# Expert layers: slots filled by rows gathered from a token table, in place of rows scattered to their slots

## What is computed

```python
x = hidden_states.reshape(-1, H)                  # 1024 x 256
logits = x @ w_gate                               # 8 experts
logits = SOFTCAP * jnp.tanh(logits / SOFTCAP)
probs = jax.nn.softmax(logits, axis=-1)
_, idx = jax.lax.top_k(probs, TOPK)               # the best 2 of 8
mask = jax.nn.one_hot(idx, E, dtype=probs.dtype).sum(-2)
weights = probs * mask
for e in range(E):
    h = jax.nn.silu(x @ w1[e]) * (x @ w3[e])      # 256 -> 512
    out = out + h @ w2[e] * weights[:, e:e + 1]   # 512 -> 256
```

## Time and profile before

| What | Value |
|---|---|
| Time, median of 3 runs | 2636.81 us (2633.54 to 2636.89) |
| Profiled execution, own time | 2635.1 us |
| Its span, first to last instruction | 2633.0 us |
| Mean granted clock of TensorE | 0.857 of full |
| First expert layer | about 62 to 257 us of the span |
| Second expert layer | about 359 to 554 us |
| TensorE busy in one expert layer | 146.3 us of 195 |
| Last slot index known to first tile transposed | 24.6 us, in either layer |

### The profile page before, as it was taken

How to read it: one execution, slowest core, us unless ns; L and a number is a source line. 1 busy time by engine, 2 the same in 40 slices (tenths; PEclk the granted TensorE clock), 3 DMA queues, 4 the chain that set the end, 5 groups by cost and what they waited for, 6 DMA issues and landing times. The chain is left out here.

```text
span 2633.0 us, 45240 instructions
## 1 busy us (share of the span) xinstructions
PE 2078.7 (79%) x16876; PEld 1605.9 (61%) x16888; DVE 1525.1 (58%) x3266; ACT 1180.3 (45%) x2905; POOL 1044.7 (40%) x965
## 2 busy tenths in 40 slices
PE   8497438978887995967798577976789676779798
PEld 5365225646565874756587466865668665546686
DVE  2222642236675335787876876868778678357432
ACT  3211421126364333853566545655556555236433
POOL 0222012220002542586535864368623767100254
PEclk9698768989998997967799588996789777989799
DMA  8422013210003303321322213222122221120430
GB/s 288 132 24 48 9 39 71 25 44 2 23 2 97 142 0 70 106 73 33 113 80 78 69 50 100 89 63 81 57 89 81 67 69 65 37 55 2 126 113 16
DMA packets 138317, 179.47 MB, mean 68 GB/s; under 512 B 62048, under 2 KB 114544, under 8 KB 132992
## 3 DMA queue, kind: packets, MB, share of 16 engines
q1 hardware_dynamic: 129952, 166.46, 20.4%
q0 software_dynamic: 8160, 10.26, 2.5%
HBM read 154.52 MB, written 22.17 MB: 67 GB/s over the span
## 5 line engine op out<-in xcount | busy, mean ns | idle before, releaser
L2695 DVE SCALAR_TENSOR_TENSOR XT<-M_delta,CW_delta,XT 128x256 f32<-128x256 f32 x576 | 249.0, 495 | 67.7 <-ACT M_delta L2475 39.7
L2146 PE MATMUL PS<-XP_delta,X 128*128 128x268 f32 (+1 forms) x1024 | 247.2, 395 | 19.8 <-DMA X<-in_L_attn_b_heads 15.6
L2146 PEld LDWEIGHTS PS<-XP_delta,X 128*128 128x128 f32 x1024 | 196.0, 193 | 71.8 <-DMA X<-in_L_attn_b_heads 19.8
L1541 PE MATMUL PS<-XP_rffn,UW_rffn 128*128 128x512 f32 x816 | 195.3, 396 | 4.6 <-POOL UW_rffn L1495 4.6
L1541 PEld LDWEIGHTS PS<-XP_rffn,UW_rffn 128*128 128x128 f32 x816 | 156.4, 192 | 38.4 <-issue 5.4
L1273 ACT ACTIVATE PR_attn<-PS,NM_attn 128x256 f32<-128x256 f32 (+1 forms) x384 | 130.8, 448 | 103.5 <-DVE NM_attn L1343 103.5
L1495 POOL TENSOR_TENSOR UW_rffn<-W_rffn,UW_rffn 128x512 fp32r<-128x512 f32 x34 | 43.7, 1286 | 301.5 <-ACT UW_rffn L1602 301.5
L561 POOL DMA_INDIRECT sums<-XS_moe,token_moe x46 | 71.7, 1559 | 221.4 <-ACT XS_moe L661 207.0
L2613 ACT ACTIVATE S_delta<-S_delta,AO_delta 128x128 f32<-128x128 f32 x512 | 159.5, 393 | 0.0
L1663 DVE TENSOR_TENSOR SU_rffn<-PS,CB_rffn 128x512 f32<-128x512 f32 x68 | 47.0, 691 | 179.4 <-PE PS L1541 157.0
L2177 PE MATMUL PS<-KQ_delta,TR_delta 128*128 128x64 f32 x1024 | 133.8, 275 | 9.6 <-ACT TR_delta L2540 8.4
(11 more groups left out here) (459 smaller groups left out, 5259.5 us busy)
## 6 DMA issues: line engine op xcount, KB each, us to landing
M_delta<-gram_delta SPq DMA_DIRECT2D x32, 1280.0 KB, 6.0
X<-in_L_attn_b_heads SPq DMA_DIRECT2D x64, 512.0 KB, 3.5
EW<-in_L_ffn_w SPq DMA_DIRECT2D x24, 512.0 KB, 10.0
CB_rffn<-routes_rffn SPq DMA_DIRECT2D x20, 512.0 KB, 21.9
XN<-in_L_attn_b_outs SPq DMA_DIRECT2D x16, 512.0 KB, 3.7
F_delta<-in_L_attn_b_outs SPq DMA_DIRECT2D x4, 2048.0 KB, 9.5
W_rffn<-in_L_ffn_tiles SPq DMA_DIRECT2D x4, 1536.0 KB, 11.5
slots<-pad SPq DMA_DIRECT2D x2, 2967.0 KB, 14.1
```

Of the source, the lines that this page charges most:

```text
L1541: last = nc.tensor.matmul(PS[:, 4 + 2 * n + q, :], UW[qw][:, r, (q * KD + k) * P:(q * KD + k + 1) * P], XP[qx][:, k, n * NB:(n + 1) * NB], ...
L2146: last = nc.tensor.matmul(PS[:, 1 + i, 0:B * (WIN - halo)], WH[:, r, i, k, :], XP[:, k, :, n * BT + halo:n * BT + WIN], start=(k == 0), st ...
L2695: nc.vector.scalar_tensor_tensor(TMP[:, r, i], RAW[:, r, i, :, tau:tau + BT], CW[:, i, h, tau:tau + 1], TMP[:, r, i], ALU.mult, ALU.add).t ...
```

## The change

`setup`, `load_experts` and `moe` change; a class `Routing` takes over the bookkeeping. `slots` is gone. XN itself is written to a tensor `rows` in HBM (1024 rows and 128 padding rows of zeros), and each tile is gathered from there by an indirect DMA that reads 128 rows by their number. For that the kernel needs a table: for each of the 128 places (lanes) in each of the 23 tiles, which token is there, and its weight. It is made as a matrix product: `spread` holds, for each of 16 columns of pairs, a 128 x 128 one-hot of the lane, `entry` a row of 23 + 23 values that are zero except at the pair's tile (row number and weight), and 16 products `spread[:, j]` x `entry[:, j]` add up the table in PSUM.

```diff
@@ load_experts
-        self.fill_slots(sp)
-        sp.dma_start(self.sums[N:N + P], self.pad[:, 0:D]).then_inc(self.zeroed, 16)
+        sp.dma_start(self.rows[N:N + P], self.pad[:]).then_inc(self.zeroed, 16)
+        sp.dma_start(self.sums[N:N + P], self.pad[:]).then_inc(self.zeroed, 16)
@@ class Routing (new): TensorE
+    def table(self, pe, spread):
+        w = (1 + self.weighted) * self.TILES
+        pe.wait_ge(self.entry_d, 1)
+        for j in range(2 * NT):
+            pe.wait_ge(self.spread_d, j // NT + 1)
+            last = nc.tensor.matmul(PS[:, 6, P:P + w], spread[:, j], self.entry[:, j].rearrange("p x t -> p (x t)"),
+                                    start=j == 0, stop=j == 2 * NT - 1)
+        last.then_inc(self.table_mm, 1)
+    def experts(self, pe):
+        pe.wait_ge(self.owner_d, 1)
+        return [pe.value_load(self.owner[0:1, t:t + 1], min_val=0, max_val=E - 1) for t in range(self.TILES)]
@@ class Routing: VectorE, behind `where` in place()
+        c.then(nc.vector.tensor_tensor(self.at_least, by_slot(self.where).broadcast_to([P, 2 * NT, t + 1]),
+                                       self.tile_at[:].unsqueeze(1).broadcast_to([P, 2 * NT, t + 1]), ALU.is_ge))
+        c.then(nc.vector.tensor_reduce(self.tiles_up[:], self.at_least, AX.X, ALU.add))
+        c.then(nc.vector.scalar_tensor_tensor(self.lo[:], self.tiles_up[:], -float(P), self.where[:], ALU.mult, ALU.add))
+    def spread(self, dve, spread, half):
+        nc.vector.tensor_tensor(spread[:, h], self.lane[:].unsqueeze(1).broadcast_to([P, NT, P]),
+                                self.lo[:, h].unsqueeze(2).broadcast_to([P, NT, P]), ALU.is_equal).then_inc(self.spread_d, 1)
+    def entries(self, dve, c):
+        nc.vector.scalar_tensor_tensor(self.value[:]..., ALU.mult, ALU.add)
+        c.then(nc.vector.tensor_tensor(self.in_tile, self.at_least[:, :, 0:t], self.at_least[:, :, 1:t + 1], ALU.subtract))
+        last = nc.vector.tensor_tensor(self.entry[:, :, 0], self.in_tile, over(self.value[:]), ALU.mult)
+        if self.weighted:
+            last = nc.vector.tensor_tensor(self.entry[:, :, 1], self.in_tile, ..., ALU.mult)
+        last.then_inc(self.entry_d, 1)
+    def tokens(self, dve, c):
+        dve.wait_ge(self.table_mm, 1)
+        if self.weighted:
+            nc.vector.tensor_copy(self.share[:], PS[:, 6, P + t:P + 2 * t])
+        c.then(nc.vector.tensor_tensor(self.token_f[:], PS[:, 6, P:P + t], self.own[:].broadcast_to([P, t]), ALU.add))
+        nc.vector.tensor_copy(self.token[:], self.token_f[:]).then_inc(self.token_d, 1)
@@ moe, SyncE
+            norm.rows_ready(sp)
+            sp.dma_start(rows, XN[:]).then_inc(rows_out, 16)
             sp.wait_ge(g_in, 16)
-            sp.wait_ge(placed, 32 * NT * (layer_no + 1))
-            for i in range(len(GROUPS) - 1):
-                at = slice(GROUPS[i], GROUPS[i + 1])
-                sp.dma_start(XS[:, at], slots[:, at]).then_inc(x_in[i], 16)
-            if layer_no == 0:
-                core.fill_slots(sp)
@@ moe, GpSimd
-            for i in range(NT):
-                for r in range(2):
-                    nc.gpsimd.indirect_dma_start(
-                        core.slots[:], bass.IndirectOffsetOnAxis(ap=slot[:, r, i:i + 1], axis=0),
-                        XW[:, r, i], None).then_inc(placed, 16)
+            def gather(t):
+                nc.gpsimd.indirect_dma_start(XS[:, t], None, core.rows[:],
+                                             bass.IndirectOffsetOnAxis(ap=token[:, t:t + 1], axis=0)).then_inc(x_in[t], 16)
+            pool.wait_ge(rows_out, 16)
+            pool.wait_ge(routing.token_d, 1)
+            for t in range(AHEAD):                      # AHEAD = 6
+                gather(t)
             for t in range(TILES):
                 pool.wait_ge(y_ev, t + 1)
                 if t or layer_no:
                     pool.wait_ge(added, 16 * (TILES * layer_no + t))
                 nc.gpsimd.indirect_dma_start(core.sums[:], ...token[:, t:t + 1]..., XS[:, t], None, compute_op=ALU.add)
+                if t + AHEAD < TILES:
+                    gather(t + AHEAD)
@@ moe, TensorE
+            routing.ranks(pe)
+            e = routing.experts(pe)
+            routing.table(pe, spread)
@@ moe, ScalarE
             norm.scalar(act)
-            norm.rows_ready(act)
-            nc.scalar.copy(XW[:, 0, :, 0:D], XN[:])
-            nc.scalar.copy(XW[:, 1, :, 0:D], XN[:]).then_inc(rows_d, 1)
+            act.wait_ge(routing.token_d, 1)             # behind exp, ahead of the loop
@@ moe, VectorE
+            routing.choose(dve, c, prob)
+            routing.place(dve, c)
+            routing.spread(dve, spread, 0)
+            routing.entries(dve, c)
+            routing.spread(dve, spread, 1)
+            routing.owners(dve, c)
+            routing.tokens(dve, c)
```

More of the change, by code:

```diff
@@ L472, in moe @@
     prob = s.sb("prob", [P, NT, E])
[L473 to L499 removed]
+    mx = s.sb("mx", [P, NT])
+    XS = s.sb("XS", [P, TILES, D])
+    spread = s.sb("spread", [P, 2 * NT, P])
     XK = s.sb("XK", [P, 3, KD, P])
@@ L676, in _ @@
             c = Chain(dve, chain_v)
-            for e in range(E):
-                nc.vector.memset(rank[:, e:e + 1], float(E - e))
-                last = nc.vector.memset(edges[:, e:e + 1], float(P * e))
-            for t in range(TILES):
-                last = nc.vector.memset(tile_at[:, t:t + 1], float(P * t))
-            c.then(last)
+            routing.tables(dve, c)
             dve.wait_ge(tanh_d, 1)
@@ L694, in _ @@
-            c.then(nc.vector.tensor_reduce(weight[:], chosen[:], AX.X, ALU.add))
-            nc.vector.tensor_copy(XW[:, :, :, D + 1], weight[:])
-            for r in range(2):
-                last = nc.vector.tensor_copy(XW[:, r, :, D], core.row_id[:, 0:NT])
-            last.then_inc(rows_d, 1)
-            dve.wait_ge(sum_mm, 1)
-            dve.wait_ge(consts, 2)
-            c.then(nc.vector.tensor_reduce(count[:], PS[:, 6, 0:NT * E].rearrange("p (i e) -> p e i", e=E), AX.X, ALU.add))
-            c.then(nc.vector.tensor_tensor(over[:], count[:].unsqueeze(2).broadcast_to([P, E, E]),
-                                           edges[:].unsqueeze(1).broadcast_to([P, E, E]), ALU.is_gt))
@@ L711, in _ @@
-            c.then(nc.vector.tensor_tensor(chosen[:], oh[:], place[:].unsqueeze(1).broadcast_to([P, 2, NT, E]), ALU.mult))
-            c.then(nc.vector.tensor_reduce(where[:], chosen[:], AX.X, ALU.add))
-            nc.vector.tensor_copy(slot[:], where[:]).then_inc(slot_d, 1)
-            c.then(nc.vector.tensor_tensor(past[:], tile_at[:].unsqueeze(2).broadcast_to([P, TILES, E - 1]),
-                                           base[:, 1:E].unsqueeze(1).broadcast_to([P, TILES, E - 1]), ALU.is_ge))
```

241 lines of the change are left out of this document (144 added, 97 removed).

## The result

| | Before | After |
|---|---|---|
| Time, median of 8 runs each | 2635.93 us (2632.6 to 2641.01) | 2643.39 us (2638.73 to 2649.43) |
| Span of the profiled execution | 2633.0 us | 2645.2 us |
| First / second expert layer, first load of one stage to first load of the next | 195.63 / 196.08 us | 202.56 / 202.69 us |
| End of `where` to first transpose, layer 1 | 24.6 us | 33.1 us |

The change made the kernel slower: after over before is 1.0039, 95% interval 1.0027 to 1.005, some 10 us (7 to 13); the two medians of the table are 7.5 us apart. 2651 was forecast, with 2641 to 2660 as the range. The two layers together are 13.5 us longer in the profiled executions (14.8 forecast); the rest of the program differs by 1.3 us the other way.

A forecast was written before the change was run, and what follows sets the result against it. The prediction took TensorE's products to bound the loop, and the wait for the first tile's transpose to decide the change. Terms sum to +7.4 us a layer, +14.8 for two, on 2635.1: 2649.9, taken as 2651 us, range 2641 to 2660.

The forecast's parts named there:

- Ahead of `where`: Before `where`, ScalarE's two copies into XW and the copies of weight and row number go: -0.8 us a layer.
- VectorE to `owner`: Behind `where`, VectorE's new operations, with `owner` last of all, add 6.1 us a layer.
- Register loads: On TensorE's queue between ranks and table, 23 loads lose their cover and add their full 15.2 us a layer.
- Table: On TensorE, 16 fp32 products, two instructions each, at half clock: +7.3 us a layer, bounds 4.2 to 8.4.
- Tokens: Behind the table, three small VectorE operations, chained once: +0.5 us a layer.
- First gather: From GpSimd's start, through the first indirect DMA, to the first transpose: +3.5 us a layer, bounds 2.6 to 4.9.
- Removed: Behind `where`, the scatters, their landing and the load back go: -24.6 us a layer.
- Second gather: Follows the first by 1.26 to 1.5 us, where the second tile came 1.24 later: +0.2 us a layer.
- rival D: Register loads run beside products and don't hold up the table, so the kernel isn't slower: 2627 us; chance 4%.
- B: The table's products bring TensorE's clock up before the loop, saving 3.5 to 4 us a layer: 2643 us; chance 14%.
- C: GpSimd's queue becomes the loop's bound as adds wait for gathers: some 2682 us, mild form 2655 to 2662; 12% for both.
- Signs forecast for the trace: Table starts when register loads end, takes 7.3 us at 0.50; first gather 0.8 us later; tiles stay 5.6 us apart.

The follow-up runs named there:

- table first with one load: Changed kernel with the table's products ahead of the register loads and one load instruction for all 23 registers; 2607.0 us, 0.9913 of before.
- loads spread: Changed kernel with tiles' experts computed right behind `where`, six register loads ahead of the table, seven behind, ten in the loop; 2612.0 us, 0.9926 of before.
- `owner` early: Changed kernel with VectorE computing the tiles' experts right behind `where`, so register loads can start earlier; 2632.5 us, 1.0004 of before.
- uncovered loads: Kernel before with one more wait: its 23 register loads also wait for the first group of XS; 2664.9 us, 1.0124 of before.
- paced gathers: Changed kernel with all 23 gathers ahead of the adds, each from the seventh waiting until the previous landed; 2671.9 us, 1.0143 of before.

## Why the prediction was right

*The path.* The prediction held that the layer's length hangs on when the first tile can be transposed. In all kernels whose loop is undisturbed the layer moves with that moment: 16.8 us sooner gives 16.8 us less (table first with one load, against after), 16.3 gives 16.7 (loads spread). (The moment is counted from `where`; a slower router, see the last section, comes on top.)

*Term by term*, layer 1, forecast and then what the rows of after show:

| Step | Forecast | Measured | From |
|---|---|---|---|
| Ahead of `where` | -0.8 | -0.6 | `where` ends 19.45 us after the stage's start (63.31), before 20.01 (62.02); the router took 4.46 us, before 4.22 |
| VectorE to `owner` | 6.1 | 6.2 | 82.76 to 89.0 |
| Register loads | 15.2 | 15.2 | 89.0 to 104.18 |
| Table | 7.3 | 7.0 | 7.03, at 0.50 |
| Tokens | 0.5 | 0.5 | 111.21 to 111.73 |
| First gather | 3.5 | 4.1 | 111.73 to 115.85 |
| Removed | -24.6 | -24.6 | |
| First tile | +7.2 | +7.9 | 52.54 us after the stage's start, before 44.61 |
| Second gather | +0.2 | 0.0 | second tile 1.27 us behind the first, before 1.27 |
| The layer | +7.4 | +6.9 | 202.56 - 195.63 |

The step on which the sign rests, register loads that lose their cover, is shown from three sides: they stand in the open in after, they make the kernel before slower by 1.2% when they are uncovered there, and the changed kernel is faster than before as soon as they are shortened, spread or put behind the table.

*The terms that were mis-sized.* The first gather: GpSimd starts 0.93 us after `token` has ended, where I took 0.3 from waits for a short VectorE operation; from its start to the transpose it took 3.19, as composed. Against that stands something the sum had at nothing: the half clock at the loop's start lasts 5.3 us behind the first transpose, before 6.7, which gives 0.7 us of TensorE time back. That isn't the table's doing: in `owner` early, whose two layers have the same code, it lasts 4.6 and 6.8 us. So this part of the agreement is luck. These two leave +7.2, and 6.9 was measured; the last 0.3 us weren't traced.

*Whole program.* Two layers give +13.5. The stage ahead of the first layer is 1.3 us longer in the profiled execution of after and a later feed-forward stage 4.4 us shorter. The 1.3 us are 16 transposes near the start that took 3.67 us in after, as long as the same ones at 0.50, and before 2.31; the profile has the granted clock at 1.00 there in both, so what made them longer stays open. Of the change the stage has only `load_experts`, without its filling of `slots`. The feed-forward stage holds nothing of it. The other stages make up 1.8 more, and the spans differ by 12.2. Over all runs it is 10.3 us (7.1 to 13.2), below my 14.8 by more than the layers of the profiled execution explain. Where the rest lies can't be read: only one execution of each kernel is traced, and that of after took 2647.0 us, 3.6 above its median. Two small slips are in the total: 2649.9 and 1.7 make 2651.6, and rival D's 2627 leaves the 1.7 out.

*Rivals.* B fell: the clock is 0.50 from the table to the first tiles in after, and with the table issued twice as well. C fell in the loop: a gather adds 0.1 us to an add's cycle. Another form of it, all 23 gathers in a row, does cost 17 us a layer, by a mechanism I hadn't named and no run shows. D, loads that run beside products, was false for this order but not in its mechanism: the loads do run beside products, those ahead of them on the queue. I had argued "one queue, in order" as if an instruction's end, not its issue, let the next one go; for the order that was forecast both read alike, for the reversed order it was wrong by 5 us (22.6 in place of 27.5).

*Signs forecast for the trace.* L540 begins when the register loads end (104.18 after 104.1), takes 7.0 at 0.50, the loop begins at 0.50, adds don't wait for DMA in it but for the last of each layer: all as written. The tiles are 5.8 apart in the middle of the loop and 5.6 at its end; I had read the 5.6 off the last adds of before, whose middle has 5.8 as well.

## What to carry to other kernels

When a change removes a long wait, list what else stood under it: here 15 us of register loads cost nothing beneath the scatters and became the largest term on the path. Put queue work such as register loads behind products that are already issued, never ahead of ones that others wait for; one swapped line turned this change from 0.4% slower to 0.3% faster, and with one load instruction for all registers to 0.9% faster. A row of indirect DMAs that is long and unbroken should be looked at in the trace, even where each of them is early.

## What the runs showed of the hardware that was not expected

- Register loads run beside products ahead of them on TensorE's queue: the first load starts at 89.0 while the table's products end at 93.0.
- A load of 23 registers takes 2.1 to 2.3 us as one instruction. Each register's operation and assertion takes about 0.29 us more, 6.6 us in all.
- The granted clock stayed 0.50 through 13.86 us of unbroken products of 46 columns, and fell from 1.00 within such products when wide ones (512 columns) had raised it.
- Single register loads took 0.30 us beside direct loads of some 350 GB/s, and up to 0.92 us right after the filling of `slots` had been started.
- ScalarE and VectorE stood still for 14 to 17 us beside 23 unbroken gathers, and not beside 17, though the stall begins when no more than 15 have been issued. Beside 12, VectorE stood still for 1.5 us in one layer and up to 2.7 in the other.
- The router's 32 instructions, which took 4.22 us before, took 6.96 to 6.97 in five layers of kernels that don't change them: the first layer with the uncovered loads and with the table issued twice, the second of `owner` early, and both with the paced gathers. One of them:

```profile
73.08 6.97 PE L700 MATMUL PS<-WG_moe,XT 128*128 128x8 f32 x32 [0.72 <-DVE XT L245]
```

  In `owner` early the clock was 0.50 through all of its second layer's router products, and in its first layer (4.07 us) it fell only near their end. So the clock moves a layer's length by close to 3 us with no change in the work; differences of that size between single traces are not evidence.
